# ScalarE's order inside an attention slot: both moves of turned probabilities ahead of both exponentials

## The reference

```python
# layer 0, second block: scores smoothed by a 3x3 kernel of its own per head and sequence
attn0 = where(mask, 0, q k^T * scale); attn = conv3x3(attn0, kernels[b, h])
p = softmax(where(mask, -inf, attn)); out = p v            # "near" (mask is causal)
# layer 0, third block: latent attention with rotated q and k, then four experts
attn = softmax(where(causal, q k^T / 4, -inf)); out = attn v  # "causal"
# layer 1, first block
attn = softmax(where(causal, q k^T / 4, -inf)); seq_out = attn v  # "tally"
return (seq_out + gated * mem_val) @ out_w.T + out_b
# layer 1, second block: each query sees 64 chosen keys, with repeats
c_sel = c_kv[b, indices]; attn = softmax(q k_sel * scale); out = attn v_sel   # "count"
```

## Time and profile before

| | |
|---|---|
| median of 3 runs | 2920.89 us (2919.4 to 2921.58) |
| the profiled execution | 2922.89 us, its span 2921.1 us |
| PE busy | 2331.1 us, 80% |
| DVE busy | 1401.0 us, 48% |
| ACT busy | 952.7 us, 33% |
| POOL busy | 366.8 us, 13% |
| granted TensorE clock, mean | 0.858 of 2.4 GHz |

### The profile page before, as it was taken

The page is one execution under the profiler, slowest core; times in us unless marked ns, Lnnn a source line. Parts: engine busy times, 40 slices in busy tenths (PEclk is TensorE's granted clock), DMA queues, the critical chain, the costliest instruction groups (busy, mean ns, idle before and its releaser), DMA issues. The chain is left out here.

```text
span 2921.1 us, 39700 instructions
## 1 busy us (share of the span) xinstructions
PE 2331.1 (80%) x13820; PEld 1661.3 (57%) x13875; DVE 1401.0 (48%) x4013; ACT 952.7 (33%) x3031; POOL 366.8 (13%) x637
## 2 busy tenths in 40 slices
PE   7677777777888887887623678888888889898988
PEld 4355555555666665675411446666666656575655
DVE  6243535354434334532129656556565555465652
ACT  3133233333433433333100234333333333343331
POOL 1040413232213041501000000000000000000000
PEclk9677777777979988798866789999999999999997
DMA  7000000001121210243450000000000000000000
GB/s 269 8 1 4 1 8 1 8 4 73 37 76 69 77 69 25 93 172 119 152 145 14 10 8 2 8 5 8 5 8 5 8 5 8 5 8 4 1 4 4
DMA packets 48462, 112.12 MB, mean 38 GB/s; under 512 B 7937, under 2 KB 30209, under 8 KB 44673
## 3 DMA queue, kind: packets, MB, share of 16 engines
q1 hardware_dynamic: 46720, 105.29, 10.4%
q0 software_dynamic: 1536, 4.20, 0.4%
HBM read 88.10 MB, written 21.36 MB: 37 GB/s over the span
## 5 line engine op out<-in xcount | busy, mean ns | idle before, releaser
L682 DVE TENSOR_REDUCE negmax<-SM 128x2 f32<-128x512 f32 x432 | 284.0, 687 | 234.2 <-PE SM L520 179.2
L638 ACT ACTIVATE PRS<-SM,negmax 128x128 f32<-128x128 f32 x608 | 250.0, 420 | 401.1 <-DVE negmax L682 399.5
L623 ACT ACTIVATE PRS<-PT 128x384 f32<-128x384 f32 (+1 forms) x512 | 264.1, 525 | 95.0 <-PE PT L556 95.0
L556 PE MATMUL PT<-const_sb,PRS 128*128 128x128 f32 x1664 | 254.9, 292 | 21.6 <-ACT PRS L623 19.2
L510 PE MATMUL SM<-KF,QM 32*128 32x256 f32 (+1 forms) x1376 | 202.9, 383 | 86.6 <-ACT PRS L636 47.6
L360 POOL TENSOR_TENSOR rstd_a<-var_a,const_sb 128x2 f32<-128x2 f32 x57 | 43.1, 756 | 1620.5 <-DVE var_a L373 998.9
L556 PEld LDWEIGHTS PT<-const_sb,PRS 128*128 128x128 f32 x1664 | 209.6, 152 | 55.5 <-ACT PRS L638 24.8
L571 PE MATMUL OA<-PRS,VS 128*32 128x256 f32 (+1 forms) x2048 | 239.5, 363 | 0.6 <-ACT PRS L623 0.6
L324 PE MATMUL PJ<-big,arena 128*128 128x256 f32 x832 | 210.7, 400 | 8.5 <-ACT big L2413 8.5
L510 PE MATMUL SM<-haloU,QM 32*128 32x128 f32 (+1 forms) x1056 | 191.8, 412 | 20.1 <-ACT PRS L638 15.8
L2249 DVE TENSOR_SCALAR arena<-arena 128x256 bf16<-128x256 bf16 x1024 | 206.2, 283 | 0.7 <-PE SC L2144 0.6
(11 more groups left out here) (481 smaller groups left out, 3834.2 us busy)
## 6 DMA issues: line engine op xcount, KB each, us to landing
arena<-lay SPq DMA_DIRECT2D x50, 1024.0 KB, 6.3
arena<-lay SPq DMA_DIRECT2D x1, 7700.5 KB, 32.3
rows<-OT SPq DMA_DIRECT2D x1, 4480.0 KB, 30.6
arena<-lay SPq DMA_DIRECT2D x1, 3862.0 KB, 19.9
rows<-OT SPq DMA_DIRECT2D x1, 3456.0 KB, 38.4
arena<-rows SPq DMA_DIRECT2D x25, 128.0 KB, 4.1
arena<-lay SPq DMA_DIRECT2D x25, 128.0 KB, 6.6
rows<-arena SPq DMA_DIRECT2D x25, 128.0 KB, 5.8
```

Source lines behind the costliest of these rows:

```text
L556: ins = pe.transpose(bank[:, o:o + P], PR[n % 4][:, t, k * P:(k + 1) * P], ident)
L623: act.activation(dst, src, ACT.Copy).then_inc(S("probs_moved"), 1)
L638: ins = act.activation(dst, src, ACT.Exp, bias=negmax[:, h, r:r + 1], accum_out=rsum[:, t, h:h + 1])
L682: st.post(dve.tensor_reduce(negmax[:, ORDER[s], :], two(banks[s % NB]), AX.X, ALU.max, negate=True), S("max_ready"))
```

## The change

In the near, causal and tally attentions ScalarE's order in a slot becomes M(2i-2), M(2i-1), E(2i), E(2i+1). The instructions, their number, their waits and all other engines' lists stay as they are. Slot 0 (no moves) and slots 8 and 9 (no exponentials) read as before, so slots 1 to 7 of 24 attentions are changed. Conv and count keep the old order.

```diff
             for i in range(attention_slots(mode)):
                 for d in range(2):
                     s = 2 * i + d - ahead
-                    if 0 <= s < H:
+                    if mode in ("conv", "count") and 0 <= s < H:
                         exponentials(s)
                     if lag <= i < PAIRS + lag:
                         move_probs(2 * (i - lag) + d)
+                for s in (2 * i, 2 * i + 1):
+                    if mode not in ("conv", "count") and s < H:
+                        exponentials(s)
```

## The result

The changed kernel takes 3008.97 us (median of 4 runs, 3003.41 to 3017.79), the kernel before 2921.1 us beside it (4 runs, 2919.4 to 2921.58): ratio 1.0305, 95% interval 1.0279 to 1.033. Slower, as forecast, but by 88 us where 63 were worked out: outside the 2966 to 3002 of the forecast's main case, and just inside its wide range of 2950 to 3010. The profiled execution took 3007.48 us, its span 3005.7 us, at a mean granted clock of 0.853 (before: 0.858). Lines from L649 on have moved down by 3: L685 is the L682 of before.

What follows compares the result with a forecast made beforehand. TensorE, waiting for ScalarE's exponentials, was taken as the bound. Terms 3.8 + 14.5 - 5.9 + 46.4 + 4 = +62.8 us on 2922.89 gave 2985.7, or 2984 as median; range 2966 to 3002, 8 times in 10 2950 to 3010.

Steps and rivals of the forecast that it cites:

- main case: Whole kernel: the summed terms hold, about 2984 us, range 2966 to 3002, chance 0.73.
- Bound and place: Layer 1: TensorE is the engine to follow; its scores wait 68.5 us for exponentials, which the change puts behind two copies.
- One clock for all slots: All changed slots: moves, exponentials and next scores timed from f, the start of a slot's six transposes.
- Near: Near attentions: unchanged at clock 1.0, S(2) 0.6 us later in slot 1 at clock 0.5; +3.8 us.
- Causal: Causal attentions: next scores 0.44 us later at 26 boundaries, 1.08 in four slots 1 at clock 0.5; sum +14.5 us.
- Ends: Ends of near and causal: last transposes wait for exponentials alone, 0.45 us less at 13 ends; -5.9 us.
- Tally: Tally attentions: later scores at uncovered boundaries, later Gelus, Exp's table load behind both moves in slot 4; +46.4 us.
- Clock: Behind tally slot 4, where TensorE idles 2.9 us: a fall of the granted clock, taken as +4 us.
- Rival C: After each of seven 2.9 us stalls in tally the next slot runs at clock 0.5: 24 us, 3004, chance 0.12.
- B: Layer 1: woven tally sequences absorb their delays, only sequence 0 of tally pays; +19 us, 2940, chance 0.08.
- D: Causal and tally: exponentials start at their maximum in spite of both moves, only gains remain; 2910 us, chance 0.05.

Runs made afterwards that it cites:

- causal_only: Kernel before with the new order in the causal attentions alone: 2943.55 us, ratio 1.0081.
- causal_filled: Kernel before with the new order in causal alone, plus twelve small matmuls in TensorE's idle times of sequences 0 to 3: 2936.23 us, ratio 1.0055.
- after_filled: Changed kernel with small zero-adding matmuls behind V in tally slots that have nothing woven in: 2994.96 us, ratio 1.0258.
- slot4_only: Kernel before with the new order in tally slot 4 of sequences 1 to 7 alone: 2956.88 us, ratio 1.0111.
- table_early: Changed kernel with one small Exp behind the feed's four Gelus, so that Exp's table loads during the hot sums: 3020.21 us, ratio 1.0332.
- near_warm: Kernel before with the new order in near alone, plus small matmuls in TensorE's idle times at the head of near attentions: 2893.75 us, ratio 0.992.
- before_filled: Kernel before with the small matmuls behind V in tally slots that have nothing woven in: 2957.69 us, ratio 1.0133.
- tally_exp_first: Kernel before with the opposite order in tally alone, both exponentials and then both moves: 2920.24 us, ratio 0.9983.

## Why the prediction was wrong, point by point

- **Bound and place**: right. S waits for exponentials, and every stall of the earlier trace rows that was forecast to grow grew.
- **One clock for all slots**: right to 0.04 us: E at f + 1.28 (1.26), S at f + 2.25 (2.24) in causal, f + 4.48 (4.46) in slot 4, and f + 3.06 (3.02) in exposed tally slots (2009.78 and 2012.84 in the changed kernel).
- **Near**: the step held (S(2) 0.6 us later), its sum did not. +3.8 was forecast and -13.1 came, the ends in it, because the clock returned to 1.0 a slot earlier. I had priced the late S(2) as if the clock's rise stood still. What moved it is not settled: it also came a slot earlier in causal_only, without a late S(2).
- **Causal**: sum too small. Sequences 0 to 3 grew by 2.83, 5.35, 3.47 and 4.29 us where 4 x 0.44 + 1.08 = 2.84 were forecast for each, 0 exact and the others above it, and 4 to 7 by 3.1 together. The excess follows the granted clock of these attentions: 0.83, 0.88, 0.88 and 0.83 before, 0.84, 0.75, 0.84 and 0.75 after. With the clock at 1.00 sequence 1 grew by 0.58 only (causal_filled).
- **Ends**: right in kind, 0.57 at the end shown where 0.45 was taken.
- **Tally**: right. 5.65 us forecast per woven attention, 5.73 or 5.74 measured where the clock is 1.00 (after_filled). In sequence 0 6.9 were forecast and 6.04 measured, but there the clock was not the same (0.88 before, 0.92 filled), so that the sums of 46.4 and 46.2 agree so closely is partly luck. The load's cost of 2.59 was 2.6 in slot4_only. The Trainium skill, "ScalarE: Activation LUTs", section "What ACT_TABLE_LOAD costs", adds 1380 ns for a drain to the 1283 ns of the load. After as before none is seen on either side of it: two moves from 1996.64 for 0.87, the load at 1997.53 for 1.28, the exponential at 1998.82.
- **Clock, the step that failed**: +4 was taken, "near the lower end" of 0 to 24, with the argument that the clock stayed at 0.96 through idle times up to 0.9 us. Measured: 25.9 us in the tally. The 0.96 was a mean over tally and count: the woven tally attentions stood at 1.00, so they had only a fall to expect. The rows I argued from had stalls of 0.28 to 0.93 us; the new ones are 1.47 us in exposed slots and 2.89 in slot 4, and I carried the steady clock over to them. With slot 4's stall alone the clock's cost was 14.1 us (slot4_only). The stalls of 1.47 us, which my price did not count at all, are enough by themselves: sequence 0 lost 5.8 us with no stall of 2.89 us in it (its five of 1.47 stand behind one of 2.24 us), and table_early, which has none anywhere, lost about 31. How many of the 25.9 us each kind costs in the changed kernel is not separated.
- **Rival C** gave 24 us and 3004, with a chance of 0.12. That its size was right is partly luck: it has a fall behind each of the seven stalls of slot 4, and the changed kernel has one behind four of them (sequences 1, 3, 5 and 7), with the others behind the shorter stalls. The rule of the Trainium skill that I set beside it ("TensorE: Matmul & The Clock Gate", section "A second HAM failure mode: psum-queue depth-cycling": idle times between groups of matmuls make the clock swing) deserved the weight that I gave to a stretch of trace whose idle times were 0.9 us at most; the clock swings in the changed kernel's rows, as by that rule.
- **B and D** are out: exposed tally slots grew in all woven sequences, and causal slots did too.

Held against the sum of 62.8 (on the span 84.6): tally's clock +21.9 over the +4; near, causal and ends together +6.0 instead of +12.4, which hid 6.4 of it by luck; and +6.6 outside near, causal and tally attentions, where nothing was forecast. That last part is the same instructions at another clock; why it comes with this sign is not settled. That the causal excess is the clock's is shown by an experiment for one sequence only.

## What to carry to other kernels

Where a change lengthens stalls of TensorE, price the clock that the work behind the stall will run at as a term of its own, and take its size from stretches with stalls of the new length or from the whole range, not from the steady stretch that the change destroys. Expect a gain or loss of a few us in stretches that you did not touch. Before giving up on an idle time of TensorE that nothing useful fits into, try a few small matmuls in it: they cost nothing where the idle time is real (after_filled, near_warm) and come into the path where it is not (before_filled). Give them a bank that nobody needs at that time, as near_warm does: the zeros that were added to a bank with open sums changed results here. And when a function table must be changed, keep its load on the side of the wait that something else covers: two instructions in front of it made 2.6 us here.

## What the runs showed that was not expected

- The granted clock can fall behind a stall of 1.47 us, with TensorE busy in the rest of its slot (2008.58 in table_early), and keep its level behind one of 2.89 us (2000.59 in the changed kernel): by these rows the length of one stall does not decide it. The same instructions with the same stall had it at 1.00 in sequence 2 and at 0.51 in sequence 3.
- Equal instructions of layer 0 took 17 us more in table_early than in the changed kernel, by the clock. The four runs of the changed kernel lie 14.4 us apart, those of the kernel before 2.2 us in the same comparison and 13.8 in the last one: differences of 0.2% need many runs here.
- A shorter attention does not pass its gain on in full: tally_exp_first saved 12.3 us in the tally and 2.6 in the time. Where the rest goes is seen (count and the parts between attentions), why it goes there is not settled.
